# Layer 2 cross-attention: row sums from the exponential, division on GpSimd ahead of the products, and the two halves of the scores apart

## The reference

```
def _L2_xattn_ref(x, context, w_qkv, w_proj, b_proj):      # x: [128, 32, 128], context: [128, 257, 256]
    NUM_HEADS = 16                                         # head width D = 8
    qkv = (x @ w_qkv.T).reshape(B, N, 3, H, D).transpose(2, 0, 3, 1, 4)
    q, k, v = (qkv[0], qkv[1], qkv[2])
    kv = context.reshape(B, N_c, 2, H, D).transpose(2, 0, 3, 1, 4)
    extra_k, extra_v = (kv[0], kv[1])
    k = jnp.concatenate([extra_k, k], axis=2)              # 257 + 32 = 289 keys
    v = jnp.concatenate([extra_v, v], axis=2)
    attn = jnp.einsum('bhnd,bhmd->bhnm', q * scale, k)
    attn = jax.nn.softmax(attn, axis=-1)
    out = jnp.einsum('bhnm,bhmd->bhnd', attn, v)
    out = out.transpose(0, 2, 1, 3).reshape(B, N, C)
    return out @ w_proj.T + b_proj
...
x = x + _L2_xattn_ref(_layernorm(x, axis=-1), ctx_2048, ...)
```

## Time and profile before

| what | us |
|---|---|
| median of 3 runs | 5422.37 |
| lowest and highest of the 3 | 5421.33, 5422.81 |
| the profiled execution, its own time | 5421.22 |
| the span of its profile | 5419.4 |
| of it the attention part of layer 2's cross-attention, first queries product to last addition | 583.8 (3512.87 to 4096.62) |

### The profile page before, as it was taken

One profiled execution on the slowest core, in us unless ns is written; L12 is line 12 of the kernel. 1 busy time (PEld: TensorE's weight loads), 2 busy tenths in 40 slices (PEclk: granted clock), 3 DMA queues, 4 the chain that ended last, 5 costly groups with the idle time before them and its releaser, 6 DMA issues. The chain is left out here.

```text
span 5419.4 us, 94009 instructions
## 1 busy us (share of the span) xinstructions
PE 4044.9 (75%) x34138; PEld 3009.2 (56%) x34138; DVE 3059.3 (56%) x5339; ACT 1992.6 (37%) x3780; POOL 726.9 (13%) x808
## 2 busy tenths in 40 slices
PE   6999999999976603699945659899993137867476
PEld 4777777777753403576633236576772125645364
DVE  1655555555556654322234456577777965867673
ACT  1333333333334400233323334366664335644222
POOL 0000000000011102100002026500001133201320
PEclk6999999999987856799976769899996568979567
DMA  2111111111101272100020023212220000000000
GB/s 62 49 47 47 47 47 47 46 45 47 44 29 59 85 83 74 57 0 0 0 48 5 0 79 126 82 57 61 61 64 3 0 5 3 0 11 1 7 0 20
DMA packets 251780, 209.82 MB, mean 39 GB/s; under 512 B 84288, under 2 KB 241953, under 8 KB 244257
## 3 DMA queue, kind: packets, MB, share of 16 engines
q1 hardware_dynamic: 251552, 206.80, 13.4%
HBM read 181.54 MB, written 24.95 MB: 38 GB/s over the span
## 5 line engine op out<-in xcount | busy, mean ns | idle before, releaser
L3324 PE MATMUL c_psO<-c_pt,c_vc 128*128 128x512 f32 x1024 | 482.2, 593 | 2.5 <-ACT c_ot L3411 2.5
L3296 PE MATMUL c_psS<-c_kc,c_qt 128*128 128x257 f32 x2048 | 465.9, 380 | 0.9 <-issue 0.9
L3296 PEld LDWEIGHTS c_psS<-c_kc,c_qt 128*128 128x128 f32 x2048 | 381.1, 190 | 66.9 <-issue 17.4
L3450 DVE COPY c_qt<-c_psQ 128x512 f32<-128x512 f32 x248 | 170.8, 689 | 399.6 <-PE c_psQ L3281 399.6
L3403 ACT ACTIVATE c_sc<-c_psS,c_mx 128x257 f32<-128x257 f32 x512 | 214.9, 472 | 486.9 <-DVE c_mx L3461 486.9
L497 PEld LDWEIGHTS f_psY<-f_w_down,f_hT 128*128 128x128 f32 x2560 | 302.8, 192 | 64.9 <-issue 51.1
L487 PE MATMUL f_psH<-f_xs,f_w_up 128*128 128x512 f32 x640 | 313.0, 626 | 18.1 <-ACT f_hT L540 18.1
L540 ACT ACTIVATE f_hT<-f_psH,f_b_up 128x512 f32<-128x512 f32 x320 | 215.1, 687 | 291.6 <-PE f_psH L487 286.9
L3281 PEld LDWEIGHTS c_psQ<-XT,c_m 128*128 128x128 f32 x1984 | 260.1, 191 | 106.2 <-issue 104.4
L497 PE MATMUL f_psY<-f_w_down,f_hT 128*128 128x128 f32 x2560 | 305.6, 276 | 10.3 <-ACT f_hT L540 7.1
L604 DVE SCALAR_TENSOR_TENSOR X<-f_psY,f_wt,X 128x128 f32 x256 | 72.1, 345 | 381.3 <-PE f_psY L497 381.3
(11 more groups left out here) (710 smaller groups left out, 8285.5 us busy)
## 6 DMA issues: line engine op xcount, KB each, us to landing
c_kc<-in_ctxT SPq DMA_DIRECT2D x128, 257.0 KB, 3.2
c_vc<-in_ctx SPq DMA_DIRECT2D x128, 256.0 KB
g_wide<-g_w_dram SPq DMA_DIRECT2D x32, 1024.0 KB, 8.2
x_kc<-in_ctxT SPq DMA_DIRECT2D x32, 512.0 KB, 3.8
x_vc<-in_ctx SPq DMA_DIRECT2D x64, 256.0 KB
l_k_dram<-l_dist SPq DMA_DIRECT2D x32, 256.0 KB, 3.0
l_q_dram<-l_turn SPq DMA_DIRECT2D x8, 1024.0 KB, 3.9
s_A<-l_k_dram SPq DMA_DIRECT2D x32, 256.0 KB, 5.9
```

Of the source, the lines that this page charges most:

```text
L3296: mm = pe.matmul(psS[:, r, 0:KEYS], qt[:, b // BT, half, b % BT, r * G:(r + 1) * G].rearrange("p h i -> p (h i)"), kc[:, b // 2 % 2, b % 2 ...
L3324: mm = pe.matmul(psO[:], vc[:, slot, c % 2, t, half * P:(half + 1) * P], pt[:, c % 2, t], start=(t == 0), stop=(t == 1))
```

## The change

The sum of each row of exponentials now comes from the exponential itself (`accum_out`), DVE takes the reciprocal of the four sums of a batch, and POOL multiplies the exponentials by it, in place, before they are turned. The products with ones go, and with them the second halves of `psO`, `om` and `nd`; `pick` writes `ot` directly, and `normal` goes. A batch is turned two batches after its scores rather than one, and its contexts follow three batches after rather than two; `sc` gets four buffers for it. PE's order is new: the two halves of the scores stand apart, with the first turning between them.

```diff
-                def scores(i, h, b, first):
+                def scores(i, h, b, half, first):
...
-                    for half in range(2):
...
                 def turn(n, c, t):
-                    if t < 2:
-                        pe.wait_ge(exp_done, (n + 1) * G)
+                    if t == 0:
+                        pe.wait_ge(scaled, n + 1)
...
-                    for which in range(2):
-                        for t in range(KT):
-                            for r in range(G):
-                                if which == 1:
-                                    val = ones[:]
-                                elif t < 2:
+                    for t in range(KT):
+                        for r in range(G):
+                            if t < 2:
...
-                    pe.wait_ge(ot_ready, m + 1)
+                    pe.wait_ge(picked, (m + 1) * G)
...
-                        scores(i, h, b, first)
+                        scores(i, h, b, 0, first)
+                        if not (first and b < 2):
+                            turn(n - 2, (b - 2) % BC, 0)
+                        scores(i, h, b, 1, first)
+                        if not (first and b < 2):
+                            turn(n - 2, (b - 2) % BC, 1)
                         if b == Q_AT and not last:
...
                             keys(i + 1, 1 - h)
-                        if not (first and b == 0):
-                            turn(n - 1, (b - 1) % BC, 0)
-                            turn(n - 1, (b - 1) % BC, 1)
+                        if not (first and b < 3):
+                            contexts(i if b >= 3 else i - 1, n - 3, (b - 3) % BC, first)
                         if not (first and b < 2):
-                            contexts(i if b >= 2 else i - 1, n - 2, (b - 2) % BC, first)
-                        if not (first and b == 0):
-                            turn(n - 1, (b - 1) % BC, 2)
+                            turn(n - 2, (b - 2) % BC, 2)
...
                 def exponentials(n, b, rows, first):
-                            act.wait_ge(turned, (n - 1) * KT)
-                        act.activation(sc[:, b % 2, r], psS[:, r, 0:NK], ACT.Exp,
-                                       bias=mx[:, b % 2, r:r + 1]).then_inc(exp_done, 1)
+                            act.wait_ge(turned, (n - 3) * KT)
+                        act.activation(sc[:, b % SC, r], psS[:, r, 0:NK], ACT.Exp, bias=mx[:, b % 2, r:r + 1],
+                                       accum_out=sm[:, b % SC, r:r + 1]).then_inc(exp_done, 1)
...
-                def invert(m, slot):
-                    v.wait_ge(picked, (m + 1) * G)
-                    v.reciprocal(rec[:, slot], nd[:, slot, 1]).then_inc(inverted, 1)
+                def invert(n, slot):
+                    v.wait_ge(exp_done, (n + 1) * G)
+                    v.reciprocal(rec[:, slot], sm[:, slot]).then_inc(inverted, 1)
...
-                    g.tensor_tensor(ot[:, slot], nd[:, slot, 0], rec[:, slot], ALU.mult).then_inc(ot_ready, 1)
+                def scale(n, slot):
+                    g.wait_ge(inverted, n + 1)
+                    g.nop(nofuse=True)
+                    g.tensor_tensor(sc[:, slot], sc[:, slot], bcast(rec[:, slot], 2, NK), ALU.mult).then_inc(scaled, 1)
```

More of the change, by code:

```diff
@@ L2149, in _ @@
                 chunk(CHUNKS - 1, 1, False, True)
[L2150 removed]
+                scale(B - 1, (BC - 1) % SC)
             @block.tensor
@@ L2271, in _ @@
                 chunk(CHUNKS - 1, 1, False, True)
-                for t in range(2):
-                    turn(B - 1, BC - 1, t)
-                contexts(CHUNKS - 1, B - 2, BC - 2, False)
-                turn(B - 1, BC - 1, 2)
+                for n in range(2):
+                    for t in range(2):
+                        turn(B - 2 + n, BC - 2 + n, t)
+                    contexts(CHUNKS - 1, B - 3 + n, BC - 3 + n, False)
+                    turn(B - 2 + n, BC - 2 + n, 2)
                 contexts(CHUNKS - 1, B - 1, BC - 1, False)
@@ L2331, in chunk @@
                             values(i, b // G, first)
-                        if not (first and b == 0):
-                            copy(n - 1, (b - 1) % BC, 0, first and b > 0)
+                        if not (first and b < 2):
+                            copy(n - 2, (b - 2) % BC, 0, first)
                         exponentials(n, b, range(G), first)
-                        if not (first and b == 0):
-                            copy(n - 1, (b - 1) % BC, 2, first and b > 0)
+                        if not (first and b < 2):
+                            copy(n - 2, (b - 2) % BC, 2, first)
                         if b == Q_AT - 4 and not last:
@@ L2351, in _ @@
                 chunk(CHUNKS - 1, 1, False, True)
-                copy(B - 1, BC - 1, 0, False)
-                copy(B - 1, BC - 1, 2, False)
+                for n in range(2):
+                    copy(B - 2 + n, BC - 2 + n, 0, False)
+                    copy(B - 2 + n, BC - 2 + n, 2, False)
             @block.vector
@@ L2404, in chunk @@
                         q = b // G
+                        if not (first and b == 0):
+                            invert(n - 1, (b - 1) % SC)
                         maxima(n, b)
@@ L2424, in _ @@
                 chunk(CHUNKS - 1, 1, False, True)
+                invert(B - 1, (BC - 1) % SC)
+                copy(B - 2, BC - 2, False)
+                pick(B - 3, BC - 3, False)
                 copy(B - 1, BC - 1, False)
@@ L2427, in _ @@
                 pick(B - 1, BC - 1, False)
-                invert(NG - 1, 1)
                 add(CHUNKS, NG - 1)
```

98 lines of the change are left out of this document (47 added, 51 removed).

## The result

The changed kernel takes 5436.32 us (median of 20 runs, 5420.38 to 5442.89), the kernel before, run beside it, 5421.93 (20 runs, 5407.3 to 5432.86). The ratio is 1.0026, 95% interval 1.0017 to 1.0034: slower by some 14 us. The forecast was 5431 within 5416 to 5452. Its total holds within that range; the terms it was made of hold only in part, and one question that it did not ask, what bounds the stage once the products with ones are gone, decides what the change is worth.

A forecast was written before the change was run, and what follows sets the result against it. PE's own work was taken to bound the stage. Plus 1.35 us a chunk made 10.8 in 8 chunks; with minus 2 for filling and draining, plus 9 on 5422.4 gave 5431 us, range 5416 to 5452.

The forecast's parts named there:

- Products with ones, minus 0.66: In PE's contexts: without the products with ones, they end 0.66 us sooner in each batch.
- A half takes as long as four products, plus 0.70: In PE's scores: two products alone take as long as four, so the separate second half adds 0.70 us a batch.
- the turnings apart, plus 0.17: On PE: turns 0 and 1 as two blocks of 0.60 instead of one of 1.03, plus 0.17 us a batch.
- the rival that hides 0.3 of the 0.87: On PE: second half's time partly hidden, added drains short; a batch of 3.64, 5393 us in all; chance 0.12.
- A batch of 3.94, plus 0.21: Plain batch by PE's own work: 3.94 us in place of 3.73, plus 0.21.
- No other engine later than PE: In a plain batch: ACT, DVE and POOL stay covered at 3.94 us; DVE's reciprocal has cover 0.35, POOL 1.5 or more.
- The three other places of a chunk: Per chunk: late exponentials minus 1.08 us, addition at group ends minus 0.7, queries' copy minus 0.53, new stall plus 0.3.
- The keys' wait: At `b` = 10: PE's wait for the queries' copy goes, as the keys' product moves behind turn 1; minus 0.53 us a chunk.
- the stall behind `qm`: At `b` = 10: DVE's `qm` delays turn 1's copy, and the next batch's first turning waits; plus 0.3 us a chunk.
- Fill and drain, minus 2: At the stage's filling and draining: one more batch, but no long reciprocal or POOL step after it; minus 2 us, bounds 0 to minus 4.
- the main case: Whole kernel: the summed terms hold, giving 5424 to 5435 us; chance 0.46.
- the first rival: In every batch: an unseen wait or longer pieces add 0.03 to 0.15 us, 5435 to 5450 us; chance 0.3.

The follow-up runs named there:

- the second product: Changed kernel with POOL's product made twice a batch, the first into a tile that nothing reads: 5483.50 us, ratio 1.0119 to the kernel before.
- Written out: Changed kernel with this stage's loop written out on all five engines, so no branch back: 5416.15 us, ratio 0.9992 to the kernel before.

## Why the prediction was right, and where it was not

- **Products with ones, minus 0.66.** Right, and shown by putting them back: 4.55 against 3.90.
- **A half takes as long as four products, plus 0.70, and the turnings apart, plus 0.17.** Right: 0.82 together in the kernel before with halves apart, 0.05 under the forecast; the turning's blocks are 0.58 to 0.59 and not 0.60, the halves 0.69 and not 0.70. Of the rival that hides 0.3 of the 0.87, 0.05 is what there was.
- **A batch of 3.94, plus 0.21.** Measured 3.90, plus 0.17. Over 128 batches the 0.04 are the 5 us by which the steady term was too large.
- **No other engine later than PE.** Right for this order: reciprocal, maxima and POOL's product are nowhere waited for in the batch. POOL's 2.35 to 2.65 was 2.11; the second product showed that its cover is real. The reduction of 370 ns and the added 0.09 to 0.10 per exponential are as worked out; maxima that stand alone take 0.76, where 0.72 stood.
- **The three other places of a chunk.** The keys' wait went, as forecast (4.76 in place of 5.16 for that batch), and the stall behind `qm` came, 0.27 where 0.3 stood. The addition came 0.09 sooner and not 0.17. With the batches a chunk grew by 0.86 inside the loop and 0.4 outside, in place of 1.35.
- **Fill and drain, minus 2.** Wrong in sign. The drain did shorten by 0.5, but the first four batches took 3.3 more. The parting brings them: with the halves together four first batches take 0.3 less than before, by their maxima. Counted from the start of the stage, the granted clock stood at 0.50 until 27.8 us; in the kernel before it was until 16.9, with the halves together until 20.3. How much of the 3.3 is the clock and how much the parting's own work was not separated; nothing in the sum had a clock in it.
- **What the sum left out.** The loop's branches back. It treated all 16 batches of all chunks as alike; the rows of before already had batches of 8.6 and 8.2 at the branches. They cost 8.5 more in the changed kernel, which is more than the whole steady term of 6.0. Written out, they are gone. At the first of them PE's idle time is 1.2 us longer, and the low clock after it 5 us longer. In the ten kernels that have the loop the low clock at a branch lasts 0 to 7 us with the halves together and 7 to 10 us with the halves apart, while PE's idle time, 2.8 to 4.5 and 3.2 to 4.2, doesn't tell them apart. Why the one and the other are longer is not settled: in the changed kernel the loads of `vc`, `vt` and `kc` are all issued from 3726.34 to 3728.88, just ahead of the branch, and before only that of `kc` (3727.46; the others end at 3723.25). Whether they delay the fetch of instructions was not tried.

So the total, 5431 against 5436, is in part luck: of its errors, 5 too much in the steady batches and 13 too little at the stage's start, its end and the branches, one hides some of the other. In the stage plus 9 was forecast and plus 18 came; the rest of the profile was 5 us shorter in the changed kernel's execution (4829 against 4834), though nothing in it was changed, so the median can't tell more. And 5436 lies just above the main case's own range (5424 to 5435), in the one that the first rival was given (5435 to 5450). That rival's reason, longer pieces or an unseen wait in every batch, did not come true: the batches were 0.04 shorter than forecast.

The step that misleads most is none of the sum. "A plain batch is PE's own work, and a change is worth what it does to that sum" was right for the kernel before by 0.08 us: a ring of 3.65 lay under 3.73. Had the change been made without parting the halves, this sentence would have forecast 3.07 and 5340, and it came to 4.05 and 5405. The parting is the step that loses: the rest of the change gains 8.5 us in the stage (585.4 to 576.9) and 16 by the medians, and the parting takes 26 and 31.

## What to carry to other kernels

Where a stage is bound by an engine at 95%, look for the rings that lie just under it, by following one batch from a release back to itself; a change that shortens the busy engine stops at the first of them, and a change that lengthens another engine's step may lift one over it. Open a ring by the order of the engine that has room (here ScalarE's copy behind one exponential) before opening it on the engine that has none. And read the batches at a loop's branch and at a stage's start apart from the middle: they can hold more than the whole steady term.

## What the runs showed of the hardware

- DVE's product of two operands from SBUF (`qm`, 128 x 2048) takes 2281 ns alone, 2.72 to 2.73 us when POOL's product runs for another 0.57 after its start, 3.84 for 1.70 (two kernels) and 4183 ns for 2.04 (POOL's product twice, of which only the second lies beside it). In all of these it ends 2.14 to 2.15 after POOL's product has ended, so it waits for the whole of it. POOL's product stays at 2.11 to 2.12 meanwhile. Maxima and copies, which read PSUM, did not change. The changed kernel escapes it because POOL has no product under way while `qm` runs.
- In the other order POOL pays. The 4286 ns of the earlier trace rows are of a product that starts while a DVE operation on SBUF runs for another 2.19 us, and it ends 2.10 after that one, in eight of eight:

```profile
4149.62 3.45 DVE L1409 TENSOR_TENSOR_SCAN r_den<-r_f 128x1024 f32<-128x1024 f32 x1 [2.15 <-ACT r_f L1353]
4150.89 4.29 POOL L1368 TENSOR_TENSOR r_e2v<-r_e,r_vv 128x992 f32<-128x992 f32 x1
```

  In all these rows the one that starts later waits, whichever engine it is on. The Trainium skill, GPSIMD Engine Reference, section "Key points", names contention between POOL and DVE's instructions with two SBUF inputs, and does not say there who pays; the prediction took it to be POOL.
- Around a branch back, where PE stood still for 2.8 to 4.5 us, the granted clock went to 0.50 (1.2 GHz) for 3 to 10 us, at all places but one (the second branch of the kernel before, 2.9 us idle). It fell 0.5 us after PE had begun again in the kernel before and 2.1 us ahead of that in the changed one, and stayed low while PE was busy for 2.00 of 2.00 us. With no branch in the stage it did not fall at these places.
- The read of the accumulator behind an exponential is 0.20 us long, and the next exponential starts 0.48 after the last in place of 0.39.
